# Attention and FFN on one core: the last sequence's first transposes behind the last scores, and two output-projection units ahead of the second rounds

## What is computed

```python
q, k, v = x @ Wq[h], x @ Wk[h], x @ Wv[h]            # per head h
attn    = softmax(causal(q @ k.T / 8))
y  = x + concat_heads(attn @ v) @ Wo                 # output projection
y  = (y - mean(y)) * rsqrt(var(y) + 1e-3) * gamma + beta
x  = layernorm(x + y)                                # eps 1e-5
h  = silu(x @ wg.T) * (x @ wu.T)                     # wg, wu, wd = integers / 127
out = layernorm(x + h @ wd.T)
```

## Time and profile before

| | |
|---|---|
| time, median of 3 runs | 1456.66 us (1456.49 to 1458.42) |
| the profiled execution's own time | 1458.17 us |
| its span from the first instruction to the last | 1456.4 us |
| mean granted TensorE clock | 0.991 of full |
| PE busy | 1409.0 us (97%) |
| DVE, ACT, POOL busy | 1031.7, 1002.1 and 984.9 us |
| the last two of 40 equal slices | PE busy in 7 and 6 tenths |

### The profile page before, as it was taken

The page is one execution under the profiler, slowest core; times in us unless marked ns, Lnnn a source line. Parts: engine busy times, 40 slices in busy tenths (PEclk is TensorE's granted clock), DMA queues, the critical chain, the costliest instruction groups (busy, mean ns, idle before and its releaser), DMA issues.

```text
span 1456.4 us, 23825 instructions
## 1 busy us (share of the span) xinstructions
PE 1409.0 (97%) x7976; PEld 1231.7 (85%) x7976; DVE 1031.7 (71%) x2747; ACT 1002.1 (69%) x1924; POOL 984.9 (68%) x926
## 2 busy tenths in 40 slices
PE   7899999999999999999999999999999999999876
PEld 6788888888888888888888888888888888888766
DVE  7777776767676766777667676776767677677864
ACT  4777777877676676867668676676767668676534
POOL 4665666556676775867768586775867768588744
PEclk9999999999999999999999999999999999999998
DMA  3323222323342132322243122132313223121000
GB/s 130 102 81 93 62 67 95 117 52 90 103 123 73 52 95 59 110 54 58 74 117 95 52 61 72 56 120 59 95 44 110 74 60 95 51 64 55 23 12 30
DMA packets 61241, 110.46 MB, mean 76 GB/s; under 512 B 16256, under 2 KB 41600, under 8 KB 61120
## 3 DMA queue, kind: packets, MB, share of 16 engines
q1 hardware_dynamic: 61120, 108.94, 25.2%
HBM read 60.95 MB, written 13.89 MB: 51 GB/s over the span
## 4 chain that ended last, share of the span: by engine, by line
PE 73%; ACT 11%; DVE 8%; POOL 4%; issue 3%; DMA 1%; SPq 0%; ACTq 0%; POOLq 0%
PE bank L798 22%; PE bank L771 15%; PE bank L671 8%; PE bank L747 8%; PE bank L734 7%; PE bank L696 5%; PE bank L833 5%; PE bank L845 3%; ACT probs_hi L987 2%; POOL probs_lo L1428 2%; ACT probs L984 2%; ACT y_tail L1023 1%; ACT Q L967 1%; POOL h_lo L1470 1%; ACT K L967 1%
## 5 line engine op out<-in xcount | busy, mean ns | idle before, releaser
L1428 POOL TENSOR_TENSOR probs_lo<-probs,probs_hi 128x512 fp32r<-128x512 f32 x576 | 747.6, 1305 | 415.1 <-ACT probs_hi L987 412.5
L984 ACT ACTIVATE probs<-bank 128x512 f32<-128x512 f32 x576 | 344.2, 598 | 299.6 <-DVE bank L1185 217.8
L771 PE MATMUL bank<-Q,K 128*128 128x512 f32 (+3 forms) x1536 | 385.9, 353 | 3.4 <-ACT probs_hi L987 2.6
L987 ACT ACTIVATE probs_hi<-bank 128x512 fp32r<-128x512 f32 x576 | 342.2, 594 | 0.0
L771 PEld LDWEIGHTS bank<-Q,K 128*128 128x128 f32 x1536 | 252.1, 190 | 33.6 <-ACT probs_hi L987 6.2
L747 PE MATMUL bank<-K,Q 128*128 128x512 f32 (+3 forms) x768 | 245.5, 362 | 3.9 <-DMA Q<-Q 3.3
L1169 DVE CUSTOM_DVE_ANT_0 bank<-bank,mask_keys_free 128x128 f32<-128x128 f32 (+3 forms) x512 | 243.2, 506 | 4.7 <-PE bank L747 4.2
L798 PE MATMUL bank<-probs_hi,VH 128*128 128x512 f32 (+3 forms) x768 | 232.6, 343 | 7.9 <-POOL probs_lo L1428 7.2
L798 PE MATMUL bank<-probs_lo,VH 128*128 128x512 f32 (+3 forms) x768 | 234.7, 346 | 0.0
L798 PE MATMUL bank<-probs_hi,VL 128*128 128x512 f32 (+3 forms) x768 | 234.7, 346 | 0.0
L1185 DVE TENSOR_TENSOR bank<-bank,mask_queries_free 128x256 f32<-128x256 f32 (+1 forms) x320 | 119.4, 373 | 129.4 <-PE bank L771 128.9
(11 more groups left out here) (173 smaller groups left out, 2230.9 us busy)
## 6 DMA issues: line engine op xcount, KB each, us to landing
Q<-Q SPq DMA_DIRECT2D x64, 256.0 KB, 3.7
K<-K SPq DMA_DIRECT2D x64, 256.0 KB, 3.6
recip_bc<-recip_scratch SPq DMA_DIRECT2D x62, 256.0 KB, 3.4
wh<-w_scratch SPq DMA_DIRECT2D x12, 768.0 KB, 4.3
wl<-w_scratch SPq DMA_DIRECT2D x12, 768.0 KB, 5.8
wo_quad<-wo SPq DMA_DIRECT2D x16, 256.0 KB, 2.9
y<-x SPq DMA_DIRECT2D x16, 256.0 KB, 3.8
x_tail<-x SPq DMA_DIRECT2D x13, 256.0 KB, 4.4
```

What stands on the lines that cost most here:

```text
L771: last = mm(bk[:, at:at + cols], KX[:, n, P * i:P * i + P], QX[:, n, q0:q0 + cols], start=(KX is K1 and at == 0), stop=(KX is K2 and at + ...
L984: A(pe_[:, g % 2, :], stb[g % 2][:, :], ACT.Exp).then_inc(exp_done, 1)
L987: A(ph[:, g % RING, :], stb[g % 2][:, :], ACT.Exp).then_inc(hi_done, 1)
L1428: G.tensor_tensor(pl[:, g % RING, :], pe_[:, g % 2, :], ph[:, g % RING, :].bitcast(F32), ALU.subtract).then_inc(lo_done, 1)
```

## The change

Four rows of the table `FINAL` are changed. The arguments of `final_at` are the steps of XB (a preparation), WO, TR, the three UP and the three DOWN; the other steps follow from these.

```diff
-FINAL = [final_at(17, 28, 33, [36, 38, 40], [38, 40, 42]), final_at(19, 30, 35, [37, 39, 41], [39, 41, 43]),
-         final_at(20, 38, 42, [44, 46, 48], [46, 48, 50]), final_at(21, 39, 43, [45, 47, 49], [47, 49, 51])]
+FINAL = [final_at(17, 28, 35, [37, 38, 40], [39, 40, 42]), final_at(19, 30, 37, [39, 41, 42], [41, 43, 44]),
+         final_at(20, 37, 42, [44, 46, 48], [46, 48, 50]), final_at(21, 38, 43, [45, 47, 49], [47, 49, 51])]
```

## The result

| | before | after |
|---|---|---|
| time, median (us) | 1456.66 (1456.49 to 1458.42, 4 runs) | 1468.49 (1466.53 to 1469.72, 4 runs) |
| the profiled execution (us) | 1458.17 | 1466.53 |
| its span (us) | 1456.4 | 1464.8 |
| mean granted TensorE clock | 0.991 | 0.987 |

The changed kernel takes 1.0077 of the time before, 95% interval [1.0065, 1.0089]: 11.2 us more (the medians differ by 11.8). The forecast was 1466.2 us, +9.5. All ratios here are of fast runs alone; one run of two_rounds_early, further down, took 2741.3 us and is left out of its ratio.

What follows compares the result with a forecast made beforehand. PE bounds most of the kernel, but hand-offs between engines set the last 80 us. Queue delays of +8.0 us plus +1.5 for TensorE's clock gave 1456.66 + 9.5 = 1466.2 us, range 1461.5 to 1470.0.

Steps and rivals of the forecast that it cites:

- Part 1: Transposes moved behind the last scores: nothing gained, 0 us, since POOL still releases the normalisation before the last exponentials.
- Part 2: WO 2 and TR 1 ahead of the first tanh: ACT held by X1 of block 1, later DVE work 3.8 us later.
- Part 5: TensorE's clock drops behind two PE pauses: +1.5 us for WO 2 with TR 1, 0 for the later stretch.
- Part 3: DVE's list after the second part of `last_norm_c1`: worked without pause, 12.27 us to the products of (0, 2).
- Part 4: The way to blocks 2 and 3: products of (2, 0) start at 1437.8 instead of 1429.84, +8.0 us at upper clock.
- the second stretch: PE work behind the pause between 1424 and 1428: 4.0 us on the path, low clock adding 0 to +2.5, taken 0.
- The clock staying up: Rival: TensorE keeps its upper level through both pauses, so only +8.0 us, 1464.7; chance 0.17.
- Hidden: Rival: DVE's DMA wait hides the change, at most one round lost, 0 to +2.6 us, 1457.9; chance 0.05.
- Faster: Rival: earlier units of blocks 2 and 3 close ACT's 3.2 us idle gap before 1427.88, 1453.5; chance 0.04.
- Slower still: Rival: low clock over both stretches and the groups of (0, 1) ahead of WO 3, +13 us, 1469.7; chance 0.08.

Runs made afterwards that it cites:

- two_rounds_early: Kernel before with WO of block 2 at step 37 and block 1's UP at 36, 37, 39, DOWN at 37, 39, 41; 1455.87 us, ratio 0.9983.
- wo_alone: Kernel before with only WO of blocks 2 and 3 one step forward (37 and 38); 1457.76 us, ratio 1.0004.
- filled_pause: Changed kernel with eight unused identity matmuls on PE ahead of WO 2; 1465.16 us, ratio 1.0047.
- tr1_before_wo2: Changed kernel with TR of block 1 at step 36 instead of 37, ahead of WO 2 on PE; 1462.07 us, ratio 1.0029.
- block1_rounds_back: Changed kernel with TR of block 1 at step 36 and block 1's UP and DOWN back at their steps before the change; 1459.27 us, ratio 1.0015.
- rounds_alone: Kernel before with only the changed UP and DOWN steps of blocks 0 and 1, TR and WO as before; 1469.18 us, ratio 1.0081.

## Why the prediction was right, point by point

**Part 1, nothing gained: right.** PE did skip the 4.33 us wait for the transposes, and waited 3.97 us for `probs_lo` instead. The normalisation of block 1 was still released by POOL (3.12 us of idle time), and the store and the DMA behind it kept their distance from the base within 0.01 us. The base did not move either: it stands 24.84 us behind DVE's L1322 of the heads before (1366.20 to 1391.04) and 24.85 in the changed kernel. What the part left out is that the zero belongs to this change and not to the transposes by themselves: with UP(0, 0) at step 36 they cost 0.2%.

**Part 2, ACT's hold: right in its mechanism and size.** X1 of block 1 was forecast 14.94 us from the base (1405.98 less 1391.04), and stands at 15.47. The second part of `last_norm_c1` was forecast done at 19.8 and was at 20.25 (1408.98 + 0.43). The forecast said 11 us of idle time on ACT; the row has 11.95. These agree partly by luck: the DMA of the row sums released DVE 1.0 us sooner than the forecast had it, and the lower clock took that back (Part 5).

**Part 3, DVE's list: right.** From the end of the second part to the products of (0, 2) it gave 12.27 us; the rows give 1421.62 - 1409.41 = 12.21.

**Part 4, the way to blocks 2 and 3: right but for the clock.** The tanh of (1, 1) was forecast 35.1 from the base and is at 35.4. X1 of block 2 was forecast at 41.2 and is at 42.6: the 24 matmuls ahead of TR 2 took 4.4 us (1426.63 to 1431.02) where 3.1 was put down. (The sum there, 1428.1 + 3.1 + 0.91, is 1432.1 and not 1432.2.) The products of (2, 0) are 9.1 us later than before, not 8.0. The forecast then had the last six rounds as long as before. They nearly are up to the last tanh: 14.59 us from the products of (2, 0), where they were 14.30. Behind it there are 10.57 us to the end and not 9.69, and 0.87 of this is the last `f_down`: 2.08 us at a granted clock of 0.50, where the same line before was

```profile
1448.22 1.21 PE L891 MATMUL bank<-w_down,K 128*128 128x256 f32 x8 [1.38 <-POOL K L1486]
```

No part of the forecast has this stretch.

**Part 5, the clock: near in its sum, wrong in how it was split.** The stillness ahead of WO 2 was forecast at some 5 us and was 2.94, because the groups of round (0, 0) ended a microsecond later than put down (8.46 from the base, their clock at 0.58 in the window 1394.20 to 1397.60) and the DMA came a microsecond sooner. The lower level followed all the same.

For WO 2 and TR 1 I took +1.5; from the start of WO 2 to X1 of block 1 are 4.07 us, where the upper clock gives 2.53, so +1.54. For the second stretch I took 0, and the rows show +1.1 (the window 1426 to 1430 has 0.72). "The pause in front of it is the shorter" was a poor reason: 3.47 us were followed by the lower level too, and it was the longer of the two. The bound of +2.5 for it, on 4.0 us of work, has no row behind it either.

Against these two stands something that no part had: the DMA of the row sums landed 1.0 us sooner in this execution (8.39 from the base and not 9.40), so that WO 2 started at 11.40 and not at 12.41. 8.0 + 1.5 + 1.1 - 1.0 is 9.6; the products of (2, 0), for which the sum was made, are 9.1 later, since the short steps of Parts 2 to 4 came out 0.5 shorter in all. The end is 10.2 later: 0.3 in the last rounds and 0.9 in the last `f_down` are added (Part 4). That the forecast of +9.5 lies so near is in part luck, since these errors go both ways.

That also bears on the difference between 10.2 by the traces and 11.2 by the ratio. A DMA that lands alike in both would bring up to 1.0 us back. But in wo_alone it released DVE at 8.35, and the tanh of (2, 0) was only 0.33 sooner than before's and the last tanh 0.31 (52.79 and 53.10), with WO 2 at the lower level; its end is later, 63.36, by the last `f_down` alone. Besides, the execution profiled before is at the upper end of its times and the one after is the lowest of its four, so a difference in the traces below that of the medians is what one would look for. How much each accounts for stays open. filled_pause tests the first stretch and gave 1.8 us in the trace, where the rows show 1.5.

By the Trainium skill, TensorE: Matmul & The Clock Gate, section Why this matters for your kernels, both pauses would cost, and the sum would be 9.5 to 12. The trace agrees at both (0.73 and 0.72), and the rule was the better guide for the second.

**The rivals.** The clock staying up falls with the window of 0.73. Hidden needed the first tanh to run before 1403, 12.0 from the base; it ran at 15.96. Faster needed the first part of `last_norm_c1` done before about 1398, 7.0 from the base; it was done at 11.30. Its price was too high as well: the idle time ahead of the tanh at 1427.88 is 1.21, 1.00 and 0.35 us, 2.56 in all, and 3.2 had counted the copy's own 0.63.

Slower still is the one that came partly true: the clock was low over all three stretches that it names (windows of 0.73, 0.55 and 0.72). But it put 5 us on them, and the path shows 1.5 and 1.1; the groups of (0, 1), 0.55, delayed nothing, since DVE came to the addition of block 3 without a wait. The measured 1468.49 lies between this rival's 1469.7 and the forecast's 1466.2.

The faster rival did name something real: rounds and WO units do interleave to a gain when the rounds stand ahead of what is held up, as in two_rounds_early. The Trainium skill, Perfetto Trace Analysis, section Optimization Strategy, on interleaving stretches with different limits, holds in that order and not in the changed one.

**What the prediction did not see.** It tells of one route. Two more lie beside it: with the hold on ACT gone, block 1's postponed rounds still cost 0.0014 (tr1_before_wo2 less block1_rounds_back, 2 us; their intervals overlap, and the traces have 2.1 us at the last tanh, 57.15 and 55.07), and the rounds' steps by themselves would have cost as much as the whole change.

## What to carry to other kernels

Where each engine works through a fixed list, a move is judged on every queue by what it puts at the head of it while something late is awaited: here four transposes, 0.6 us together, behind a late unit left ACT idle for 12 us, and the order of two instructions on ACT gave back 6 of 11 us by the times, 3 by the traces. Work that doesn't need the late result goes ahead of it on all engines alike, which gave 0.17% here; the parts of such a change can't be priced one by one and added (0.04, 0.20 and 0.81% alone, 0.77% together). In a tail of hand-offs a pause on TensorE can cost once by its length and again in the work behind it, so a pause ahead of a critical group is worth filling, up to its end. It need not cost: in wo_alone the times show nothing of it.

## What the runs showed of the hardware

- WO 2, four matmuls of 128x256 (f32), which the trace records as eight: 3.59 us behind 2.94 us of stillness, 1.97 us behind 0.94 us. Elsewhere 3.47, 3.83 and 2.85 us of stillness were followed by the lower level (windows of 0.72, 0.54 and 0.57), and 0.62 by 1.00. All of these pauses are shorter than the two of before that the prediction had read (4.33 and 4.53 us on PE; the 3.6 us window shows only part of the second).
- The length of the pause alone does not decide. In filled_pause 2.23 us were followed by a group of 2.07 us, but 2.62 us by one of 1.21, where the same group behind 2.62 us took 2.05 in the changed kernel. The last `f_down`, behind 1.36 to 1.39 us in every trace, took 2.07 or 2.08 us in six of thirteen and 1.21 or 1.22 in seven.
- The same row-sum DMA chain, issued 3.5 us from the base before and after, released DVE at 9.40 and 8.39 us from the base, and at 8.35 in wo_alone. The difference is in its first half: the second DMA (L545) is issued 3.01 us behind the first (L541) before, 1.95 after and 2.09 in wo_alone (3.85 in rounds_alone, where DVE was released at 10.29). A microsecond of what a single trace shows in this place may be such a spread.
- The profiled execution after was ahead of that of before by 2.34 us at 64 us, by 1.89 at DVE's L1322 just ahead of the tail, and by 1.88 at the base. By the spans alone the change looks like +8.4 us, by the common base like +10.2.
